# GpSimd's low parts in a cross-attention and expert kernel: three casts of cover in the prologue, tiles 6 and 8 in each batch

## The reference, cut to what matters

```python
kv = context @ Wkv; k, v = split(kv); q = layernorm(x) @ Wq
dots = einsum('bhnd,bhmd->bhnm', q, k) * SCALE - (1 - mask) * MASK_NEG
x = x + (softmax(dots) @ v) @ Wout + bout            # heads merged
h = gelu(einsum('etd,edf->etf', layernorm(x), w1) + b1)   # one expert per batch
x = x + einsum('etf,efd->etd', h, w2) + b2
```

## Time and profile before

| | us |
|---|---|
| median of 3 executions (384.51, 385.98, 385.91) | 385.91 |
| the profiled execution, device time | 386.91 |
| its span, first to last instruction | 385.0 |
| PE busy in the span | 367.7 (96%) |
| DVE busy | 284.7 (74%) |
| ACT busy | 255.0 (66%) |
| POOL busy | 116.4 (30%) |

### The profile page before, as it was taken

How to read it: one execution, slowest core, us unless ns; L and a number is a source line. 1 busy time by engine, 2 the same in 40 slices (tenths; PEclk the granted TensorE clock), 3 DMA queues, 4 the chain that set the end, 5 groups by cost and what they waited for, 6 DMA issues and landing times.

```text
span 385.0 us, 5782 instructions
## 1 busy us (share of the span) xinstructions
PE 367.7 (96%) x1713; PEld 280.6 (73%) x1713; DVE 284.7 (74%) x456; ACT 255.0 (66%) x334; POOL 116.4 (30%) x125
## 2 busy tenths in 40 slices
PE   6899999999999999999999999999999999999794
PEld 6667777777677877777777777777777876787563
DVE  5798667978797679878797679787788678343653
ACT  3455577697669476696679466787678456958421
POOL 1520573246224350246034341336142420022000
PEclk9899999999999999999999999999999999999988
DMA  6685269329832772359834591269546450376100
GB/s 241 219 171 168 46 118 209 82 86 167 196 80 80 146 174 52 84 126 238 193 86 121 96 211 38 82 149 257 126 109 139 90 107 6 109 144 120 24 2 6
DMA packets 30622, 47.10 MB, mean 122 GB/s; under 512 B 2011, under 2 KB 21371, under 8 KB 30608
## 3 DMA queue, kind: packets, MB, share of 16 engines
q0 software_dynamic: 9936, 27.40, 36.4%
q1 hardware_dynamic: 20672, 19.52, 16.5%
HBM read 24.59 MB, written 0.23 MB: 64 GB/s over the span
## 4 chain that ended last, share of the span: by engine, by line
PE 79%; DVE 11%; issue 5%; DMA 2%; ACT 1%; SPq 1%; DVEq 0%
PE ps_s L439 26%; PE ps_a L479 22%; PE ps_x L496 10%; PE ps_a L472 7%; PE ps_x L529 4%; DVE chunk_max L899 2%; PE ps_a L416 2%; PE ps_x L549 2%; DMA ctxt_raw<-in_ctx_t 2%; DVE ex_lo L895 2%; DVE shift_diag L910 1%; DVE ex_sum L889 1%; PE ps_x L453 1%; PE ps_x L558 1%; PE ps_x L511 1%
## 5 line engine op out<-in xcount | busy, mean ns | idle before, releaser
L899 DVE TENSOR_REDUCE chunk_max<-ps_x 128x1 f32<-128x500 f32 x168 | 110.8, 676 | 32.3 <-PE ps_x L496 29.2
L697 ACT ACTIVATE ex_all<-ps_s 125x896 f32<-125x896 f32 x96 | 88.1, 918 | 48.5 <-PE ps_s L439 46.6
L479 PE MATMUL ps_a<-ex_all,ctx_sb 125*128 125x448 f32 x248 | 110.9, 540 | 0.0
L715 ACT COPY ps_s<-shift_row 125x896 f32<-125x896 f32 x94 | 85.7, 911 | 12.5 <-DVE shift_row L1036 10.0
L496 PE MATMUL ps_x<-ctxt_hi,qk_hi 128*128 128x500 f32 x168 | 82.0, 490 | 4.7 <-DVE chunk_max L899 3.6
L1213 POOL DMA_DIRECT2D ex_all<-ex_all x48 | 42.4, 884 | 119.6 <-ACT ex_all L697 116.4
L439 PE MATMUL ps_s<-qk_hi,ctxt_hi 128*125 128x448 f32 x192 | 76.4, 479 | 0.0
L479 PEld LDWEIGHTS ps_a<-ex_all,ctx_sb 125*128 125x128 f32 x248 | 46.2, 189 | 17.2 <-issue 12.8
L439 PE MATMUL ps_s<-qk_lo,ctxt_hi 128*125 128x448 f32 x192 | 54.8, 367 | 0.0
L439 PE MATMUL ps_s<-qk_hi,ctxt_lo 128*125 128x448 f32 x192 | 54.8, 366 | 0.0
L439 PEld LDWEIGHTS ps_s<-qk_hi,ctxt_hi 128*125 128x125 f32 x192 | 35.9, 187 | 24.5 <-issue 22.8
(11 more groups left out here) (108 smaller groups left out, 402.7 us busy)
## 6 DMA issues: line engine op xcount, KB each, us to landing
ex_all<-ex_all POOLq DMA_DIRECT2D x48, 448.0 KB, 4.8
ctxt_raw<-in_ctx_t SPq DMA_DIRECT2D x8, 750.0 KB, 6.0
ctx_sb<-in_ctx SPq DMA_DIRECT2D x8, 750.0 KB
ctxt_hi<-in_ctx_t POOLq DMA_DIRECT2D x21, 250.0 KB, 3.0
w_sb<-in_w SPq DMA_DIRECT2D x4, 512.0 KB, 4.9
w_sb<-in_w SPq DMA_DIRECT2D x8, 256.0 KB, 7.0
ex_all<-in_wq_t SPq DMA_DIRECT2D x2, 256.0 KB, 3.8
ex_all<-in_wk_t SPq DMA_DIRECT2D x2, 256.0 KB, 4.9
```

The source lines that it names most:

```text
L479: mm = nc.tensor.matmul(ps_a[:, c, 0:CH], ctx_sb[0:MT, u, t, :], ex(t)[0:MT, c * CH:(c + 1) * CH], start=(slot == 0), stop=(slot == TM - 1))
L697: nc.scalar.activation(half(ex(t)[0:MT, :]), src, ACT.Exp, scale=SCALE).then_inc(ex_ready, 1)
L715: nc.scalar.copy(ps_s[0:MT, t % 2, :, 0:CH], half(shift_row[0:MT, b.parity, :])).then_inc(seeded, 1)
L899: nc.vector.tensor_reduce(chunk_max[:, k, t:t + 1], filled()[:, 0:MC], AX.X, ALU.max).then_inc(job_free, 1)
```

## The change

- Prologue: the first chunk of `ctxt_lo` of batch 0 waits until all three casts of `ctxt_hi` are done, not for its own alone (the two others then find their wait met).
- Tile 6 on POOL: `ctx_lo` of the next batch is made here, behind chunk 1, and no longer at tile 7.
- Tile 8 on POOL: chunk 2 is made here, no longer at tile 7, and behind a new wait for the third `ex_lo` of the batch (that of tile 6).
- ACT casts `ctx_hi` of the next batch at tile 5 in place of 6.

```diff
-    SPLITS, CTX_HI_AT = len(SPLIT), 6
+    SPLITS, CTX_HI_AT = len(SPLIT), 5
...
             def ctxt_lo_chunk(b, k):
                 if b.i is None and b.off == 0:
-                    pool.wait_ge(ctxt_hi_ready, k + 1)
+                    pool.wait_ge(ctxt_hi_ready, KM)
...
                         pool.wait_ge(ex_lo_ready, b.at(SPLITS, 2))
                         ctxt_lo_chunk(b.later(1), 1)
-                    if prepare and t == 7:
+                        ctx_low_part(b.later(1))
+                    if prepare and t == 8:
+
+                        pool.wait_ge(ex_lo_ready, b.at(SPLITS, 3))
                         ctxt_lo_chunk(b.later(1), 2)
-                        ctx_low_part(b.later(1))
```

## The result

| | before | changed |
|---|---|---|
| median of 20 executions each (us) | 384.61 | 381.29 |
| range | 382.52 to 386.40 | 379.17 to 385.00 |
| profiled execution | 386.91 | 381.56 |
| its span | 385.0 | 379.6 |

The ratio of the executions is 0.9902 with a 95% interval of 0.9883 to 0.9921: by it the change makes the kernel 3.8 us faster (3.0 to 4.5). The two medians alone differ by 3.3 us. The ratio leaves out the slowest execution of the changed kernel (385.00), which counts as slow. Forecast were 3.9 us and 382.0, with a range of 380.3 to 383.8.

The account below looks back on a forecast made before the run. PE was taken to bound the kernel, busy 367.7 of 385.0 us, with waits for DVE held up by POOL. Gains of 3.33 + 0.6 = 3.9 us from 385.91 gave 382.0, range 380.3 to 383.8.

Parts of the forecast that it names:

- PE stands once per loop batch at tile 8, because DVE stood behind POOL.: Tile 8, six loop batches: PE idles about 0.25 us (plain) or 0.65 us (pair); ex_lo of tile 6 waited out ctx_lo.
- Plain batch 0.41 us: Tile 8 of each of three plain batches: PE regains its lost pace, 0.41 us, limited by PE.
- Pair batch 0.70 us, limited by DVE: Tile 8 of each of three pair batches: DVE is 0.70 us earlier, so PE gains 0.70 of 0.81 us.
- The sum of these, 3.33 us: Loop batches: 3 x 0.41 + 3 x 0.70 = 3.33 us, with bounds of 2.7 and 3.7; batch 0 gains 0.
- "I take 0" for SP's later load: Tile 8: ctxt_raw load moves from 95.8 to about 98.9, beside that tile's add, which still lands in time; cost 0.
- DVE idle before L889 ended by a DMA: Sign of being wrong in the profile after: a DVE wait at that line that a DMA ends; no size given.
- rival (d): Tile 8: ctxt_raw load delays the add; over 8.5 us landing decides; up to 6.5 us slower, 392.4; chance 0.04.
- The prologue's 0.6 us: Prologue: negpen ends at 13.06 in place of 13.67, so the max job at 14.53 comes 0.6 us earlier.
- Rival (a), the clock: Prologue: with a shorter PE gap the clock stays at 2.4 GHz, priced 1.3 us, giving 380.7; chance 0.22.
- (b): Rival at tile 10: PE's wait for the shift gives back the pair batches' 3 x 0.70 us, giving 384.1; chance 0.14.
- (c): Rival at tile 8: exclusion is not what delays DVE, only the prologue's part stays, giving 385.3; chance 0.07.

Follow-up runs that it names:

- chunk 2 at tile 7: Changed kernel with POOL's chunk 2 back at tile 7 without the new wait, ctx_lo still at tile 6: 380.53 us, ratio 0.9905; again on another chip 381.08 us, 0.9918.
- the tile parts alone: Changed kernel with the old prologue wait, each chunk waiting for its own cast only: 382.26 us, ratio 0.9925 against the kernel before.
- The part alone: Kernel before with only the prologue's new wait, all three casts first: 384.18 us against 385.02, ratio 0.9986.
- filling the gaps: Kernel before with 3 and 4 spare matmuls in PE's two prologue gaps: 384.86 us against 385.04, ratio 0.9995.
- the run with the cast at tile 6: Changed kernel with ACT's cast of ctx_hi back at tile 6 in place of 5: 382.70 us, ratio 0.9941 against the kernel before.

## Why the prediction was right

- **PE stands once per loop batch at tile 8, because DVE stood behind POOL.** Shown: with POOL's two operations moved, `ex_lo` is 1.17 us at most in every profile, PE's waits there are gone, and it is at that place of each batch that the changed kernel gains its lead.
- **Plain batch 0.41 us.** It measured 0.48 to 0.56. The step to the late job gained 0.42; the rest is that the late job, which started after idle time, took 0.11 us longer (0.50 against 0.39 us), a term that I had not counted.
- **Pair batch 0.70 us, limited by DVE.** At tile 8 the lead grew by 0.67 to 0.71 us in the profile with chunk 2 at tile 7. Right.
- **The sum of these, 3.33 us.** With no DMA wait it is 3.66 to 3.79 (chunk 2 at tile 7); in the three profiles of the changed kernel 2.76, 3.36 and 3.55, and 3.28 with the tile parts alone.
- **"I take 0" for SP's later load.** This step failed, and what the prediction had named as a sign of being wrong, DVE idle before L889 ended by a DMA, did occur. Two things in it were off. The price of 0 took the landings of one batch for all; in the other two plain batches of the same trace they were up to 8.3 us. And the limit of 8.5 us worked out for rival (d) was too high: DVE reached its sum 7.9 us behind the issue of the add in the first plain batch and 7.7 us in the two others. I had let the add go out earlier by the gain, but the exponential of tile 8, which releases it, lies ahead of the place of the gain (its lead in batch 1 is 0.01 us, that of tile 9 is 0.57). So adds of 8.0 to 8.7 us were enough, eight times in four profiles. DVE stood 0.6 to 2.0 us in one execution of the changed kernel, and against "chunk 2 at 7" 0.2 to 1.0 us of it reached the end; PE did not pay all of it.
- **The prologue's 0.6 us.** As a term of each execution this is wrong. The cast of 1.46 us is met only in some executions of before. The part alone gave 0.84 us of median, with an interval that holds zero. Where the cast was held up, the third max job came 14.53 - 13.35 = 1.18 us earlier, of which 0.36 is an earlier first cast, so 0.82; at the first exponential it is 2.1 to 2.4 us, counted from the first cast. Where it was not, the change costs 0.2 us. That the average of these lies near 0.6 is luck.
- **Rival (a), the clock.** Between the two profiled executions its picture fits: the low stretch of the earlier trace rows is absent in the changed kernel's, and of the 5.4 us between the spans 2.7 lie in the prologue, some 1.5 of them in that stretch (1.3 was the price). It is no gain of each execution: filling the gaps left the median of before where it was (0.9995), and low stretches come and go in both kernels. The stretch behind the third max job was seen with a held cast alone.
- **Rivals (b) and (c)** are out: the gain of the pair batches passes tile 10 (0.69 us at tile 8, 0.63 at the next batch), and POOL was what delayed DVE.

The errors have different signs, a few tenths each: the load took some of the gain away, and the plain batches made up for some of it. That is part of why 3.9 met 3.8, and the interval of 3.0 to 4.5 would have hidden it in any case.

## What to carry to other kernels

Find where the bounding engine stands and ask whether the engine it waits for ran or stood: a row far over its own median, ending one normal duration after another engine's row, is exclusion. Moving the other operation repays what the bounding engine lost, or what the blocked engine lost where that is less: here 0.5 us in plain batches, limited by PE, and 0.7 in pair batches, limited by DVE. Move the least that clears the overlap: every operation moved later drags the DMA behind it, and every one left waiting in a queue holds up the DMAs issued behind it. Before a collision or a landing time is priced for every batch and every execution, read it in each batch of the profile, and look at a second profile.

## What the runs showed of the hardware that was not expected

- Cutting POOL's subtraction into four instructions let DVE in between them in plain batches (1.56 us) and not in pair batches (2.18 to 2.20 us), in all three of each kind, in one profile.
- A POOL subtraction's row is 1.56 to 1.60 us long right behind a DMA issue of POOL, or behind a row of that kind, and 1.30 us where POOL idled before it (54.01 in the run with the cast at tile 6). This is no slower work: in the earlier trace rows they begin 0.28 to 0.35 us before the row ahead of them ends. The two of the earlier trace rows end at 95.59 and 96.83, 1.25 us apart. So POOL's rows are to be compared by their ends.
- Executions of the same program differ in who loses a collision, by about a hundredth of a microsecond: POOL's first chunk starts 0.51 us after the first cast in the two profiles in which DVE is held up (1.46 us), and 0.50 in the two in which POOL is (1.67 us).
